# FFN stage of a fused attention and FP4 kernel: the down product in three passes of high and low parts, with the scales of h's blocks in gapped rows

## The reference

```python
def fp4_linear(x, w):
    xq = fp4_quant_dequant(x)
    wq = fp4_quant_dequant(w)
    return jnp.einsum('bsk,nk->bsn', xq, wq)
gate = fp4_linear(x, w_gate)
y = fp4_linear(x, w_up)
h = jax.nn.silu(gate) * y
return fp4_linear(h, w_down)
```

## Time and profile before

| | |
|---|---|
| median of three runs | 1844.01 us |
| profiled execution, own time | 1844.23 us |
| its span, first to last instruction | 1842.5 us |
| PE busy over the span | 1760.6 us (96%) |
| DVE | 1448.3 us (79%) |
| POOL | 1396.5 us (76%) |
| ACT | 1064.8 us (58%) |
| 250 to 300 us: PE / DVE / POOL / ACT busy | 49.86 / 48.10 / 23.12 / 16.36 us |
| 250 to 300 us: granted TensorE clock | 1.00 |

### The profile page before, as it was taken

One profiled execution on the slowest core, in us unless ns is written; L12 is line 12 of the kernel. 1 busy time (PEld: TensorE's weight loads), 2 busy tenths in 40 slices (PEclk: granted clock), 3 DMA queues, 4 the chain that ended last, 5 costly groups with the idle time before them and its releaser, 6 DMA issues.

```text
span 1842.5 us, 29200 instructions
## 1 busy us (share of the span) xinstructions
PE 1760.6 (96%) x10596; PEld 1088.6 (59%) x10596; DVE 1448.3 (79%) x2034; ACT 1064.8 (58%) x1334; POOL 1396.5 (76%) x688
## 2 busy tenths in 40 slices
PE   6979999968999999999999999999999999999889
PEld 4768999944555555555555555555555555554589
DVE  7978999978788878887888788778877887884353
ACT  4642333315666666666666666666666666667531
POOL 3863544415898989999989899999899999999800
PEclk9999999988999999999999999999999999999899
DMA  8651221121233342332224322333433233322574
GB/s 290 238 201 43 73 105 38 47 72 46 73 86 89 93 139 85 88 89 86 85 90 127 104 85 88 87 86 86 127 94 100 84 90 85 87 73 77 186 264 154
DMA packets 164591, 195.11 MB, mean 106 GB/s; under 512 B 48352, under 2 KB 112736, under 8 KB 164192
## 3 DMA queue, kind: packets, MB, share of 16 engines
q1 hardware_dynamic: 164448, 193.25, 33.5%
HBM read 133.69 MB, written 59.51 MB: 105 GB/s over the span
## 4 chain that ended last, share of the span: by engine, by line
PE 61%; DVE 21%; issue 6%; POOL 2%; DMA 2%; ACT 1%; SPq 0%; DVEq 0%; POOLq 0%; ACTq 0%
PE banks L1025 19%; PE banks L1003 15%; PE banks L945 11%; PE banks L979 8%; PE banks L1546 3%; DVE half_max L1069 3%; PE banks L1008 3%; PE banks L1034 2%; DVE h_scales L110 2%; DVE banks L1103 2%; POOL acc L1189 2%; DMA o_in<-o_scratch 2%; DVE f_y L131 2%; DVE f_amax L109 2%; DVE f_y L134 2%
## 5 line engine op out<-in xcount | busy, mean ns | idle before, releaser
L1189 POOL TENSOR_TENSOR acc<-acc,prob 128x1024 f32<-128x1024 f32 x384 | 919.0, 2393 | 78.9 <-ACT prob L1228 46.7
L1069 DVE TENSOR_REDUCE half_max<-banks 128x2 f32<-128x1024 f32 x512 | 627.2, 1226 | 217.9 <-PE banks L979 215.5
L1228 ACT ACTIVATE prob<-banks 128x1024 f32<-128x1024 f32 x512 | 509.8, 1023 | 397.5 <-PE banks L1008 389.8
L1025 PE MATMUL banks<-prob,v 128*64 128x512 f32 x2048 | 495.7, 605 | 0.0
L1240 ACT ACTIVATE banks<-max_all 128x1024 f32<-128x1024 f32 x256 | 263.4, 1029 | 15.3 <-DVE half_max L1069 3.4
L1025 PEld LDWEIGHTS banks<-prob,v 128*64 128x64 f32 x2048 | 124.4, 136 | 227.6 <-issue 189.9
L979 PE MATMUL banks<-k_hi,q_hi 64*128 64x512 f32 x1024 | 232.1, 451 | 17.8 <-DVE half_max L1069 16.2
L979 PEld LDWEIGHTS banks<-k_hi,q_hi 64*128 64x128 f32 x1024 | 96.5, 186 | 233.5 <-issue 125.9
L1189 POOL TENSOR_TENSOR acc<-prob,prob 128x1024 f32<-128x1024 f32 x64 | 153.8, 2402 | 91.9 <-ACT prob L1228 91.9
L945 PE MATMUL banks<-xT,wqk 128*128 128x512 f32 x768 | 217.3, 419 | 2.1 <-DVE k_lo L1112 2.1
L1003 PE MATMUL banks<-q_hi,k_hi 64*128 64x512 f32 x1024 | 204.3, 395 | 8.7 <-ACT prob L1228 8.7
(11 more groups left out here) (121 smaller groups left out, 2138.5 us busy)
## 6 DMA issues: line engine op xcount, KB each, us to landing
max_all<-max_scratch SPq DMA_DIRECT2D x64, 512.0 KB, 4.1
v_scratch<-v_out SPq DMA_DIRECT2D x32, 512.0 KB, 2.6
wqk<-wp_scratch SPq DMA_DIRECT2D x32, 512.0 KB, 3.8
v<-v_scratch SPq DMA_DIRECT2D x32, 512.0 KB, 5.9
inv_rows<-inv_scratch SPq DMA_DIRECT2D x128, 128.0 KB, 3.3
o_scratch<-o_norm SPq DMA_DIRECT2D x64, 256.0 KB, 2.2
o_in<-o_scratch SPq DMA_DIRECT2D x8, 2048.0 KB, 11.2
xn_scratch<-p_xT SPq DMA_DIRECT2D x32, 256.0 KB, 2.9
```

What stands on the lines that cost most here:

```text
L1025: ins = nc.tensor.matmul(o_ps[head * DH:(head + 1) * DH, :], v[s % 2][:, kt, at:at + DH], prob[n % SLOTS][:, head, :], start=kt == 0, stop ...
L1069: nc.vector.tensor_reduce(half_max[:, half % 2, :, t % GRP, part], guess_bank(s, i), axis=AX.X, op=ALU.max, negate=True).then_inc(half_max ...
L1189: nc.gpsimd.tensor_tensor(acc[b][:, :, :], first, prob[n % SLOTS][:, :, :], ALU.add).then_inc(added, 1)
L1228: nc.scalar.activation(prob[n % SLOTS][:, :, :], s_ps[n % 2][:, :, :], ACT.Exp).then_inc(exp_done, 1)
```

## The change

The down product becomes three passes over high and low parts, like the other products of the kernel. `hT` and a new tile `wd_hl` get a high and a low half. ACT's copy of h now gives the high part, a new VectorE instruction `low_h` gives the low part (PSUM minus high part), and PE waits for that. The weights' parts are made once, at the start of the stage, by ACT and POOL. The scales of a tile of h are stored as 11 rows of 4 with one unused word behind each, and the working tiles shrink from 1024 to 704 columns. The core of the diff:

```diff
 def spread(ap):
 
-    return ap.unsqueeze(2).to_broadcast([P, ap.shape[1], BLOCK16])
+    n = len(ap.shape)
+    return ap.unsqueeze(n).to_broadcast([*ap.shape, BLOCK16])
...
-    amax, scale, inv, raw = (tmp[k][:, 0:nb] for k in (0, 1, 2, 5))
+    amax, inv, raw = (tmp[k][:, 0:nb] for k in (0, 2, 5))
+    scale = tmp[1] if len(tmp[1].shape) == 3 else tmp[1][:, 0:nb]
...
-    scales = sb("h_scales", [P, 2, FF // BLOCK16], F32)
+    scales = sb("h_scales", [P, 2, FF // BLOCK16 // GRP, GRP + 1], F32)
...
-    hT = sb("hT", [P, FT, P], F32)
+    hT = sb("hT", [P, 2, FT, P], F32R)
+    wd_hl = sb("wd_hl", [P, 2, FT * D], F32R)
...
-        return tmp[0], scales[:, t % 2, :], *tmp[2:], tmp[2]
+        return tmp[0], scales[:, t % 2, :, 0:GRP], *tmp[2:], tmp[2]
...
+        def low_h(n):
+
+            dve.wait_ge(h_high, n + 1)
+            to, src = h_parts()
+            nc.vector.tensor_tensor(to[:, LO], src, to[:, HI].bitcast(F32), ALU.subtract).then_inc(h_low, 1)
...
-                for step in (scaled, masked, bounded):
+                chain.link(scaled(), (lambda: low_h(n - 2)) if n >= 2 else None)
+                for step in (masked, bounded):
                     chain.link(step())
...
         groups(dve, group)
+        low_h(TILES - 2)
+        low_h(TILES - 1)
...
+        pool.wait_ge(wd_high, 1)
+        nc.gpsimd.tensor_tensor(wd_hl[:, LO, :], wdT[:, :], wd_hl[:, HI, :].bitcast(F32), ALU.subtract).then_inc(wd_low, 1)
         groups(pool, group)
...
+        nc.scalar.activation(wd_hl[:, HI, :], wdT[:, :], ACT.Copy).then_inc(wd_high, 1)
         silu(0)
...
         def turn_h(n):
             pe.wait_ge(hq_ready, n + 1)
+            if not (type(n) is int and n == 0):
+                pe.wait_ge(h_low, n)
...
         def down(n):
-            pe.wait_ge(h_high, n + 1)
+            pe.wait_ge(h_low, n + 1)
...
             for j in range(FT):
-                ins = nc.tensor.matmul(down_ps[:, 0:D], hT[:, j, :], wdT[:, j * D:(j + 1) * D], start=j == 0, stop=j == FT - 1)
+                for hs, ws in PARTS:
+                    ins = nc.tensor.matmul(down_ps[:, 0:D], hT[:, hs, j, :], wd_hl[:, ws, j * D:(j + 1) * D],
+                                           start=k == 0, stop=k == 3 * FT - 1)
```

More of the change, by code:

```diff
@@ L127, in round_steps @@
     cols = src.shape[1]
-    scale, inv = (a[:, 0:cols // BLOCK16] for a in tmp[1:3])
+    inv = tmp[2][:, 0:cols // BLOCK16]
+    scale = tmp[1] if len(tmp[1].shape) == 3 else tmp[1][:, 0:cols // BLOCK16]
     y, m = (a[:, 0:cols] for a in tmp[3:5])
@@ L521, in ffn_part @@
     NG = TILES // GRP
-    tmp = tuple(sb(f"f_{name}", [P, GRP * D // n], F32)
+    tmp = tuple(sb(f"f_{name}", [P, FF // n], F32)
                 for name, n in (("amax", BLOCK16), ("scale", BLOCK16), ("inv", BLOCK16), ("y", 1), ("m", 1)))
-    scales = sb("h_scales", [P, 2, FF // BLOCK16], F32)
+    scales = sb("h_scales", [P, 2, FF // BLOCK16 // GRP, GRP + 1], F32)
     wp_in = sb("wp_in", [P, 2, DC * WP], F32)
@@ L540, in ffn_part @@
     wp_high, wp_low, wo_high = sem("wp_high"), sem("wp_low"), sem("wo_high")
+    wd_high, wd_low, h_low = sem("wd_high"), sem("wd_low"), sem("h_low")
     h_summed, h_rounded, pad_zero = sem("h_summed"), sem("h_rounded"), sem("pad_zero")
@@ L560, in h_tmp, with h_parts @@
     def h_tmp(t):
-        return tmp[0], scales[:, t % 2, :], *tmp[2:], tmp[2]
+        return tmp[0], scales[:, t % 2, :, 0:GRP], *tmp[2:], tmp[2]
+    def h_parts():
+        return hT, turn[:, 0:FPAD].rearrange("p (c n) -> p c n", c=FT)
     def x_parts(t):
@@ L673, in high_h @@
                 act.wait_ge(down_done, n)
-            nc.scalar.activation(hT[:, :, :], turn[:, 0:FPAD].rearrange("p (c n) -> p c n", c=FT),
-                                 ACT.Copy).then_inc(h_high, 1)
+            to, src = h_parts()
+            nc.scalar.activation(to[:, HI], src, ACT.Copy).then_inc(h_high, 1)
         def silu(n):
@@ L745, in down @@
         def down(n):
-            pe.wait_ge(h_high, n + 1)
+            pe.wait_ge(h_low, n + 1)
             if not (type(n) is int and n == 0):
                 pe.wait_ge(res_ready, n)
+            else:
+                pe.wait_ge(wd_low, 1)
+            k = 0
             for j in range(FT):
-                ins = nc.tensor.matmul(down_ps[:, 0:D], hT[:, j, :], wdT[:, j * D:(j + 1) * D], start=j == 0, stop=j == FT - 1)
+                for hs, ws in PARTS:
+                    ins = nc.tensor.matmul(down_ps[:, 0:D], hT[:, hs, j, :], wd_hl[:, ws, j * D:(j + 1) * D],
+                                           start=k == 0, stop=k == 3 * FT - 1)
+                    k += 1
             ins.then_inc(down_done, 1)
```

## The result

The changed kernel takes 1856.62 us (median of four runs, 1855.93 to 1859.38), against 1843.19 (1841.36 to 1844.02) for the kernel before, in the same session. The ratio is 1.0076, with a 95% interval of 1.0061 to 1.0091: slower. A later session gave 1854.62 (1853.71 to 1857.59) against 1841.82, ratio 1.0071 [1.0058, 1.0084]. The forecast was 1847.8, slower or the same, in a range of 1843 to 1858: the sign is right, the time is inside the range, and the size is short by 8.8 us. The profiled execution took 1855.93 us (span 1854.1), 11.7 more than that of before.

The account below looks back on a forecast made before the run. It took DVE, averaging 7.38 us a tile, to bound the FFN loop, with POOL's round trip next. Loop +2.82 and end +0.71 make 3.53 us on 1844.23: 1847.8, range 1843 to 1858.

Parts of the forecast that it names:

- The main case: FFN loop: POOL's round trip takes the place of the lock; 1847.8 us, own range 1845 to 1851, chance 0.66.
- the rival in which POOL's `hq` slows down: POOL's L136 slows to 1.70 us with three-level scale strides, loop 0.31 longer 31 times; 1857.4 us, chance 0.12.
- the new loop: FFN plain tile, end of L134 to the next: POOL 3.32, hop 0.10, DVE 2.94 plus 0.75, together 7.11 us.
- The weights' parts: Stage start: ACT's copy 1.5 us, POOL's subtraction about 3.6, both hidden; uncovered, at most 1 us, once.
- The gap: Scale steps L110 and L111 no longer held, 0.22 us each; rival that one stays held: 1867 or 1861, chance 0.10.
- POOL's round trip wasn't shorter than its rows: Rival for the FFN loop: round trip shorter than recorded, PE or DVE the bound; put at 1838 us, chance 0.12.
- `h` waiting for the SiLU: Sign in the FFN loop: DVE's L583 waiting for ACT's SiLU would make PE the bound.
- POOL's extra work: FFN tiles with extra POOL instructions: L131 held, 0.99 us each of eight times and 2.07 us twice.
- The loop's +2.82: FFN stage, L134 of tile 0 to that of tile 31: end moves from 377.94 to 380.76, +2.82 us.
- comes to the down product about there and waits 0.2 us: PE in each FFN tile: waits 0.2 us for `low_h` before the down product, all hidden.
- the term of the end, +0.71: Last down product, tile 31: `low_h` 0.95 plus hop 0.07 come in, product 2.20 instead of 2.51; +0.71 us.
- a length that moves by more than 2 us: Sign of being wrong: an attention stage whose own length moves by more than 2 us.

Follow-up runs that it names:

- Experiment 1: Changed kernel with the gap taken away, scales of h stored as 44 in a row again: 1873.64 us, ratio 1.0160.
- experiment 2: Changed kernel with `low_h` of tile n-2 moved ahead of L134, behind the reciprocal: 1835.21 us, ratio 0.9953.
- experiment 3: Kernel before with the gapped scales alone, down product in plain fp32: 1835.14 us, ratio 0.9960.
- Experiment 5: Changed kernel with the last three tiles as before (plain fp32 down product, no `low_h`): 1846.66 us, ratio 1.0025.
- experiment 10: Changed kernel with 40 added transposes keeping PE busy through its wait at the stage's end: 1849.54 us, ratio 1.0039.
- experiment 7: Changed kernel with `low_h` behind the reciprocal, the last three tiles as before, and two `f_y` tiles: 1827.91 us, ratio 0.9920.
- 8: Kernel before with the gapped scales and two `f_y` tiles, down product in plain fp32: 1836.44 us, ratio 0.9965.
- experiment 4: Changed kernel with two `f_y` tiles, so L134 of tile n needs POOL's tile n-2 only: 1835.86 us, ratio 0.9965.

## Why the prediction was right, and where it fell short

**The time in the range: in part luck.** The main case had 1847.8, with a range of its own from 1845 to 1851, and 1856.6 lies outside that. The range of the whole forecast reached to 1858 for the sake of the rival in which POOL's `hq` slows down (1857.4), and that did not happen. The direction and the new loop were right for the reason given; the size was not.

**The tile: right.** L112 and L113 at 0.20 (0.22 from start to start was taken), `low_h` at 0.95 as worked out, L134 idle for POOL 0.44, POOL's round trip as the new loop at 7.11 where 7.11 was the sum. The weights' parts were hidden as worked out: ACT's copy took 1.48 us, POOL's subtraction 3.48, and it ended at 142.83, before DVE's first work on h at 143.46. PE's product takes 2.25 where 2.20 was taken, which is hidden in the loop. Experiment 1 shows the gap's part, experiment 2 that of `low_h`'s place.

**Rivals out.** POOL's `hq` with gapped scales costs 1.40, so that rival (1.70) is gone. The price in the Trainium skill that was weighed against it (GPSIMD Engine Reference, "7. Performance pitfalls for Q7 kernels", for reads with a step over 8 bytes) doesn't show here: 0.01 us a tile, where the estimate from it was 0.59. Its remedy speaks of the inner step, as the prediction said, and there nothing changed. The gap did what it was taken to do. POOL's round trip wasn't shorter than its rows. One sign was read wrongly, though: `h` waiting for the SiLU was to show PE as the bound, for the kernel before and after. In experiment 3 PE sets the pace from tile 17 on, and `h` waits for no SiLU there; POOL waits for PE's transposes instead. That sign alone could not rule PE out. For the changed kernel experiment 2 does.

**POOL's extra work: right.** 8.12 - 7.11 = 1.01 for a tile with L627 (0.99 predicted), and 9.20 - 7.11 = 2.09 for `low_wo` (2.07).

**The loop's +2.82 became +4.13.** 0.9 us of the rest is tile 9, 8.02 us long instead of 7.11. L134 of tile 8 took 2.98 us, held by `low_wo`, so `low_h` came late and PE stood still. The same happened in tile 12 with the other `low_wo`. Both in order of time, with the windows of the two products (columns as above):

```profile
207.66 3.54 PE L779 MATMUL banks<-wd_hl,hT 128*128 128x256 f32 x18 [2.09 <-DVE hT L590]
211.00 1.27 PE L766 MATMUL banks<-ident,hq 128*128 128x128 f32 x6
...
240.10 2.41 PE L779 MATMUL banks<-wd_hl,hT 128*128 128x256 f32 x18 [2.09 <-DVE hT L590]
242.34 0.82 PE L766 MATMUL banks<-ident,hq 128*128 128x128 f32 x6
```

```profile
208.00:212.00 4.00, 4.00 (x23) 4.00 (x22) 3.83 (x8) 0.38 (x1) 1.69 (x1) 0.57 0.00 0
240.00:244.00 4.00, 3.90 (x31) 3.90 (x32) 3.90 (x7) 1.18 (x3) 1.81 (x2) 1.00 0.15 53
```

The wait is the same 2.09 us both times, but only the first time did the clock fall: the product took 3.34 us there and 2.24 in the second place, where the clock stayed at 1.00 and tile 13 took its 7.12. So the 0.9 us are the clock's, not the wait's. Another 0.3 is tile 31 (7.43), whose L134 starts 0.46 behind the end of POOL's L139 instead of 0.10; no run tells why. That PE "comes to the down product about there and waits 0.2 us" was right for a plain tile and not for these.

**The failed step is the term of the end, +0.71.** It measured 5.38 - 0.26 = +5.12. The step took the end of the kernel before and put `low_h` and a hop between ACT and the last down product. Without saying so, it kept the start of the transposes of tile 31 where it was, right behind POOL. At the end PE has no gate and up product to fill the time, so each of the last three down products waits for its own `low_h`. The times from the last L137 on show it: `hq` of tile 31 is there after 6.00 us, before after 4.18 (+1.8, POOL waited 1.94 for PE); the transposes start 2.67 later, before 0.05 (+2.6); and the down product 2.71 behind them, before 1.77 (+0.9, the only part in the forecast). Experiment 5 took all of it away. The two +1.8 and +2.6 hold 2.3 us of clock, by experiment 10.

**The rest, +2.0 in the attention and output, stays open.** It is just what the prediction had named as a sign of being wrong, a length that moves by more than 2 us. But it is within what these parts vary between executions of one kernel (from the second `rotate` on 1455.7 and 1457.4 for the changed one), so it may be no effect of the change. No run tells.

## What to carry to other kernels

Where an engine frees itself from a lock, look at what it then waits for, and put new work into that wait: `low_h` behind the waiting instruction cost 21 us more than the same `low_h` in front of it. Walk through the last two or three tiles of a pipelined stage by themselves, waits in order, since there every new handoff counts in full and PE can lose its clock while it waits. And a part that makes one engine cheaper pays only together with the parts that make it the bound: the three-pass product was worth 8 us with the others in place (experiment 7 against 8), and the kernel that has it without them (experiment 1) was 30 us slower than the kernel before.

## What the runs showed of the hardware that was not expected

- In experiment 4 a DVE instruction that was already held went ahead of POOL's next one: L134, whose record starts 0.27 us before that of POOL's L629, ran at the end of L139, and L629 took 1.94 us instead of 1.30. In the changed kernel L134 started 0.15 us behind POOL's L627, and DVE was held instead, 1.90 for 0.89. In both the one that started first went first, so tenths of a microsecond decided it, and it was worth 1.0 us a tile.
- A hold shows as a long duration, not as idle time: L112 ends 0.05 behind POOL's instruction (44 columns), L134 0.75 behind it (704).
- Behind idle times of PE of 4.36 and 2.09 us the granted clock of the next stretch was 0.50 and 0.57; 18 matmuls took 4.01 and 3.34 us in place of 2.25. Behind another idle time of 2.09 us it was 1.00, and they took 2.24: a wait of that length may or may not cost the clock.
